# Selection masks by comparison on VectorE, indices in memory of their own, and a new order of the work around the turn, in a four-layer graph kernel

## What is computed

```python
s = jnp.sort(jnp.where(nd[..., None], x[:, None, :, :], jnp.inf), axis=2)
nv = nd.sum(2)
for tau, w in zip((0.25, 0.5, 0.75), (0.25, 0.5, 0.25)):
    pos = tau * jnp.maximum(nv - 1, 0)
    lo, hi, frac = floor(pos), ceil(pos), pos - floor(pos)
    v_lo, v_hi = s[lo], s[hi]          # taken along axis 2
    agg = agg + w * (v_lo + frac * (v_hi - v_lo))
out = x + agg
y = (relu(out @ W1 + b1) @ W2 + b2) * mask
```

## Time and profile before

| | before |
|---|---|
| time, median of 3 runs | 3453.47 us (3452.79 to 3454.65) |
| profiled execution | 3456.97 us, its span 3455.2 us |
| granted TensorE clock, mean of the span | 0.846 of full |
| PE busy | 2531.8 us, 73% |
| PE weight loads | 1180.9 us, 34% |
| DVE busy | 2743.5 us, 79% |
| ACT busy | 2210.2 us, 64% |
| chain that ended last | PE 44%, DVE 29%, ACT 17%, issue 7%, DMA 2% |

### The profile page before, as it was taken

The page is one execution under the profiler, slowest core; times in us unless marked ns, Lnnn a source line. Parts: engine busy times, 40 slices in busy tenths (PEclk is TensorE's granted clock), DMA queues, the critical chain, the costliest instruction groups (busy, mean ns, idle before and its releaser), DMA issues.

```text
span 3455.2 us, 48310 instructions
## 1 busy us (share of the span) xinstructions
PE 2531.8 (73%) x17616; PEld 1180.9 (34%) x17770; DVE 2743.5 (79%) x5221; ACT 2210.2 (64%) x3296; POOL 13.7 (0%) x24
## 2 busy tenths in 40 slices
PE   0000015688989888888989898888888898986996
PEld 0000003233333434333434333343334343333765
DVE  7999998886869788787878796878778787735776
ACT  2112434578777787878778787878777877761232
POOL 0000000000000000000000000000000000000000
PEclk6555557799999999999999999999999999997777
DMA  3002000001010101011010101010100101010011
GB/s 65 0 0 61 6 0 21 10 19 20 19 20 22 30 9 32 13 31 20 19 20 19 20 19 26 15 30 11 34 10 29 20 19 20 2 27 25 26 36 37
DMA packets 157564, 74.67 MB, mean 22 GB/s; under 512 B 125192, under 2 KB 140698, under 8 KB 157082
## 3 DMA queue, kind: packets, MB, share of 16 engines
q1 hardware_dynamic: 153210, 70.68, 8.8%
q10 hardware_dynamic: 4128, 1.05, 0.2%
HBM read 42.27 MB, written 16.83 MB: 17 GB/s over the span
## 4 chain that ended last, share of the span: by engine, by line
PE 44%; DVE 29%; ACT 17%; issue 7%; DMA 2%; SPq 0%; ACTq 0%; DVEq 0%
PE rows L621 10%; PE ring L584 8%; PE found_bank L631 6%; ACT hot L1043 5%; PE bcast L597 4%; ACT below L1008 3%; DVE keys L1305 2%; DVE keys L1306 2%; PE bcast L702 2%; PE bcast L711 2%; PE bank L873 2%; ACT prod L1036 2%; DVE delta L1347 1%; DVE delta L1345 1%; DVE perm L1349 1%
## 5 line engine op out<-in xcount | busy, mean ns | idle before, releaser
L1043 ACT ACTIVATE hot<-bcast,consts 128x1024 bf16<-128x1024 f32 x744 | 832.4, 1119 | 189.6 <-PE bcast L597 188.9
L621 PE MATMUL rows<-hot,table 128*64 128x512 bf16 x4608 | 681.2, 403 | 0.0
L584 PE MATMUL ring<-member,neigh_t 128*128 128x512 bf16 x1924 | 502.3, 402 | 61.1 <-ACT words L1000 28.7
L1036 ACT ACTIVATE prod<-rows 128x512 f32<-128x512 f32 x720 | 432.8, 601 | 46.3 <-PE rows L621 46.1
L631 PE MATMUL found_bank<-prod,consts 128*64 128x512 f32 x1536 | 410.5, 612 | 0.0
L597 PE MATMUL bcast<-idx_t,consts 32*128 32x512 f16 x1488 | 305.2, 407 | 104.9 <-ACT hot L1043 102.3
L610 PE MATMUL rows<-fine_rows,consts 32*128 32x512 bf16 x768 | 305.0, 397 | 28.5 <-DMA fine_rows<-fine_t 28.5
L521 PE MATMUL ring<-identb,adj_b 128*128 128x128 bf16 x256 | 34.6, 263 | 386.3 <-ACT adj_b L928 375.1
L584 PEld LDWEIGHTS ring<-member,neigh_t 128*128 128x128 bf16 x2048 | 187.0, 102 | 370.2 <-issue 110.2
L621 PEld LDWEIGHTS rows<-hot,table 128*64 128x64 bf16 x4608 | 210.8, 111 | 262.3 <-issue 191.3
L597 PEld LDWEIGHTS bcast<-idx_t,consts 32*128 32x128 f16 x1488 | 70.6, 91 | 491.4 <-ACT hot L1043 360.7
(11 more groups left out here) (348 smaller groups left out, 4580.9 us busy)
## 6 DMA issues: line engine op xcount, KB each, us to landing
late<-in_adj_dram SPq DMA_DIRECT2D x16, 1024.0 KB, 5.5
fine_rows<-fine_t SPq DMA_DIRECT2D x512, 24.0 KB
adjt_d<-neigh_t SPq DMA_DIRECT2D x16, 512.0 KB, 2.7
adj_l<-adjt_d SPq DMA_DIRECT2D x16, 512.0 KB, 3.6
adj_s<-adjt_d SPq DMA_DIRECT2D x16, 512.0 KB, 3.5
parts_d<-parts SPq DMA_DIRECT2D x6, 512.0 KB, 5.3
table<-parts_d SPq DMA_DIRECT2D x192, 16.0 KB, 2.2
xt_d<-keys SPq DMA_DIRECT2D x2, 1024.0 KB, 9.2
```

The source lines that it names most:

```text
L584: ins = mm(ring[u % 2][:, :], kept_t[:, j, P * i:P * i + P], member[:, j, n // 2, 512 * (n % 2):512 * (n % 2) + 512], start=(j == 0), stop ...
L621: ins = mm(rows[u % 2][C * h:C * h + C, :], table[:, s, GROUPS * h + g8, :], hot[:, u % HOT, h, :], start=False, stop=(s == 2), skip_group ...
L1036: run(prod[:, u % DEEP, :], rows[u % 2][:, :], ACT.Relu).then_inc(S["prod_by_act"], 1)
L1043: run(hot[:, u % HOT].rearrange(flat), spread_bank(l, u)[0][:, 0:2, :].rearrange(flat), ACT.Relu, bias=eq_bias[:, :]).then_inc(S["hot_read ...
```

## The change

ACT's masks go, with `edge`, `limit_ready` and `mask_made`; DVE makes them by a comparison in `select`, in a single buffer. The indices get `idx_home`, so the wait for the turn leaves tile 0 and stands in `bits_start` of the next graph. To make room fine_t, adj_l and hid_t share `turned`. The turn begins with the first fine block. SP sends fine_t in 64 DMAs instead of 32: 16 with one run per partition for plane 0 (four semaphores), then 16 for plane 1, and, when all three fine blocks are there, 32 with two runs; the ninth unit waits for the last 48 together, and adj_l is loaded after all of them. The chunks of the next first tile stand between the last units: 0 and 1 behind unit 43, then two behind each of units 44 to 46. PE sums tile 0 right behind the turn. The units are spread evenly over each tile (`share`), 22 lie in the select part, and limits(p) comes ahead of bits_last.

The core of the diff; declarations, the prologue's masks and ACT's matching order of the interleaved chunks are left out:

```diff
-LEAD = (0, 5, 10, 15, 20)
+LEAD = (0, 4, 9, 14, 22)
 SUM_AT = (4, 5, 6, 4)
 LATE = LEAD[NT]
-STEP = [LATE + n for n in (0, 1, 2, 4, 6, 7, 9, 11, 13, 15, 16, 18, 21, 23, 26, 28)]
+STEP = [LATE + n for n in (0, 1, 2, 4, 6, 7, 9, 11, 13, 14, 15, 17, 19, 21)]
 UNITS = K * GROUPS
 TURNS = K + K // 2
 BY_VECTOR = ()
 ROW_GROUP = (3, 1, 0, 2, 0, 2, 1, 3)
 ROW_SLOT = (0, 0, 0, 0, 1, 1, 1, 1)
+TURN_ORDER = (K, 0, K + 1, K + 2, 1, 2, 3, 4, 5)
...
+def share(i, s):
+
+    return LEAD[i] + (LEAD[i + 1] - LEAD[i]) * (s + 1) // 10
...
-        below = sb("below", [P, 2, TAUS, G * C], BF16)
+        below = sb("below", [P, TAUS, G * C], BF16)
...
-        idx_at, temps_at = 0, 3 * NT * K * C
-        idx = pool12[:, idx_at:idx_at + 2 * NT * K * C].bitcast(F16).rearrange("p (t k b d e) -> p t k b d e", t=NT, k=K, b=4, d=2)
-        idx_b = pool12[:, idx_at + 2 * NT * K * C:idx_at + 3 * NT * K * C].bitcast(BF16).rearrange("p (t n) -> p t n", t=NT)
+        temps_at = 3 * NT * K * C
+        idx_home = sb("idx_home", [P, 3 * NT * K * C], U16)
+        idx = idx_home[:, 0:2 * NT * K * C].bitcast(F16).rearrange("p (t k b d e) -> p t k b d e", t=NT, k=K, b=4, d=2)
+        idx_b = idx_home[:, 2 * NT * K * C:].bitcast(BF16).rearrange("p (t n) -> p t n", t=NT)
         idx_t = sb("idx_t", [P, K, N], F16)
-        fine_t = sb("fine_t", [P, 2, K // 2, N], BF16)
+        turned = sb("turned", [P, K * N], BF16)
+        fine_t = turned[:, :].rearrange("p (s q n) -> p s q n", s=2, n=N)
+        adj_l = turned[:, 0:NT * N].rearrange("p (t n) -> p t n", t=NT)
+        hid_t = turned[:, NT * N:].bitcast(F32)
...
+            def fine_part(g8, n, s, lo, hi):
+
+                slots_of = fine_rows[:, :, :].rearrange("p (q s e) n -> p q s e n", s=2, e=2)
+                row, to = s * C + 8 * g8, 32 * ROW_GROUP[g8] + 8 * n
+                return sp.dma_start(slots_of[to:to + 8, lo:hi, s, ROW_SLOT[g8], :], fine_t[row:row + 8, n, lo:hi, :])
+
             def place_fine(l):
 
-                hold(sp, S["idxT_ev"], TURNS * l + TURNS, S["sp_passed"])
+                hold(sp, S["idxT_ev"], TURNS * l + 1, S["sp_passed"])
                 if l == 0:
                     sp.wait_ge(S["cdone"], 4)
-                slots_of = fine_rows[:, :, :].rearrange("p (q s e) n -> p q s e n", s=2, e=2)
+                for g4 in range(4):
+                    for g8 in (2 * g4, 2 * g4 + 1):
+                        for n in range(2):
+                            fine_part(g8, n, 0, 0, 1).then_inc(fine_in[g4], 16)
+                for g8 in range(GROUPS):
+                    for n in range(2):
+                        fine_part(g8, n, 1, 0, 1).then_inc(S["later_in"], 16)
+                hold(sp, S["idxT_ev"], TURNS * l + 4, S["sp_passed"])
                 for s in range(2):
                     for g8 in range(GROUPS):
-                        row, to = s * C + 8 * g8, 32 * ROW_GROUP[g8]
                         for n in range(2):
-                            sp.dma_start(slots_of[to + 8 * n:to + 8 * n + 8, :, s, ROW_SLOT[g8], :],
-                                         fine_t[row:row + 8, n, :, :]).then_inc(fine_in[s][g8], 16)
+                            fine_part(g8, n, s, 1, 3).then_inc(S["later_in"], 16)
+                hold(sp, S["later_in"], 768 * l + 768, S["sp_passed"])
+                for g4 in range(4):
+                    hold(sp, fine_in[g4], 64 * l + 64, S["sp_passed"])
...
-                if u < 2 * GROUPS:
-                    pe.wait_ge(fine_in[k][g8], 32 * l + 32)
+                if u < GROUPS and u % 2 == 0:
+                    pe.wait_ge(fine_in[u // 2], 64 * l + 64)
+                if u == GROUPS:
+                    pe.wait_ge(S["later_in"], 768 * l + 768)
...
-                for u in range(TURNS):
+                for u, k in enumerate(TURN_ORDER):
...
-                units(l, 2)
                 if not b:
                     for n in range(4):
                         chunk(b, 1, n)
+                sum_first(b, 0)
+                units(l, 1)
+                sum_size(b, 0)
                 chunk(b, 1, 4)
+                units(l, 2)
+                chunk(b, 1, 5)
+                chunk(b, 1, 6)
                 units(l, 3)
-                chunk(b, 1, 5)
-                sum_first(b, 0)
-                sum_size(b, 0)
-                chunk(b, 1, 6)
+                chunk(b, 1, 7)
                 units(l, LEAD[1])
-                chunk(b, 1, 7)
                 for i in range(1, NT):
                     for s in range(10):
                         if i + 1 < NT and s < CW:
                             chunk(b, i + 1, s)
-                        units(l, min(LEAD[i] + (s + 1) // 2, LEAD[i + 1]))
+                        units(l, share(i, s))
...
-                    units(l, STEP[14])
                     pe.wait_ge(S["nv_read"], p + 1)
                     chunk(p, 0, 1)
-                    chunk(p, 0, 2)
-                    units(l, STEP[15])
-                    for n in range(3, CW):
+                for n in range(2, CW, 2):
+                    units(l, STEP[13] + n // 2)
+                    if p is not None:
                         chunk(p, 0, n)
+                        chunk(p, 0, n + 1)
...
-                    wait(act, S["mask_made"], NT * b + i - 1)
+                    wait(act, S["cnt_read"], NT * b + i - 1)
...
-            def mask(b, i, k):
-
-                if k == 0:
-                    act.wait_ge(S["limit_ready"], b + 1)
-                    act.wait_ge(S["cw_ev"], NT * CW * b + CW * i + 2)
-                    wait(act, S["mask_used"], NT * b + i - 1)
-                ins = run(below[:, i % 2, k, 0:(G - 1) * C], cnt2[:, i % 2, 0:(G - 1) * C], ACT.Sigmoid,
-                          bias=edge[:, i, k:k + 1], scale=-STEEP)
-                if k == 2:
-                    ins.then_inc(S["mask_made"], 1)
...
-                units(l, 3)
                 chunk(b, 1, 2)
                 chunk(b, 1, 3)
-                mask(b, 1, 0)
+                units(l, 3)
+                keep_sums(b, 0)
+                chunk(b, 1, 4)
                 units(l, 4)
-                chunk(b, 1, 4)
+                chunk(b, 1, 5)
+                chunk(b, 1, 6)
                 units(l, 5)
-                chunk(b, 1, 5)
-                mask(b, 1, 1)
-                keep_sums(b, 0)
-                chunk(b, 1, 6)
-                units(l, 6)
                 chunk(b, 1, 7)
-                mask(b, 1, 2)
+                units(l, LEAD[1] + 2)
                 for i in range(1, NT):
-                    level = LEAD[i] + 2
                     for s in range(10):
-                        if i + 1 < NT:
-                            if s == 2:
-                                mask(b, i + 1, 0)
-                                units(l, min(level + 1, LEAD[i + 1] + 2))
-                                mask(b, i + 1, 1)
-                                mask(b, i + 1, 2)
-                            if s < CW:
-                                chunk(b, i + 1, s)
-                        units(l, min(level + (s + 1) // 2, LEAD[i + 1] + 2))
+                        if i + 1 < NT and s < CW:
+                            chunk(b, i + 1, s)
+                        units(l, share(i, s) + 2)
...
                 for k in range(TAUS):
                     did(ts(starts[:, k, 0:last], cnt[:, 0:last], above[:, i, k:k + 1], None, ALU.is_equal))
+                for k in range(TAUS):
+                    did(ts(below[:, k, 0:last], cnt[:, 0:last], limit[:, i, k:k + 1], None, ALU.is_le))
...
+                need(count[0])
+                v.engine_nop().then_inc(S["cnt_read"], 1)
                 units(l, LEAD[i + 1])
                 need(count[0])
                 wait(dve, S["sums_ps"], 2 * (NT * b + i))
-                dve.wait_ge(S["mask_made"], NT * b + i + 1)
-                if i == 0 and b:
-                    dve.wait_ge(S["idxT_ps"], TURNS * b)
...
-            def bits_start():
-
+            def bits_start(t_of):
+
+                if t_of:
+                    dve.wait_ge(S["idxT_ps"], TURNS * t_of)
...
                     members(p, 3)
+                    limits(p)
                 units(l, STEP[12])
                 if t_of is not None:
                     bits_last()
                 if d is not None:
                     gcn_end(d)
-                if p is not None:
-                    limits(p)
```

More of the change, by code:

```diff
@@ L320, in build @@
         S = {n: sem(n) for n in names}
-        fine_in = [[sem(f"fine_in{s}_{g8}") for g8 in range(GROUPS)] for s in range(2)]
+        fine_in = [sem(f"fine_in{n}") for n in range(4)]
         adjs_in = [sem(f"adjs_in{q}") for q in range(SLOTS)]
@@ L1144, in region @@
                     chunk(p, 0, 0)
-                if d is not None:
-                    root_of(d, 2)
-                units(l, STEP[14] + 2)
-                if p is not None:
                     chunk(p, 0, 1)
-                    chunk(p, 0, 2)
-                units(l, UNITS + 2)
-                if p is not None:
```

(30 more changed lines are left out.)

28 lines of the change are left out of this document (12 added, 16 removed).

## The result

| | before | after |
|---|---|---|
| time, median of 4 runs | 3454.06 us (3452.79 to 3456.51) | 3520.47 us (3512.53 to 3525.06) |
| ratio to before, with its 95% interval | | 1.0189 (1.0169 to 1.0209) |
| profiled execution, its span | 3456.97 us, 3455.2 us | 3512.53 us, 3510.7 us |
| granted TensorE clock, mean | 0.846 | 0.834 |
| PE busy / DVE busy / ACT busy | 2531.8 / 2743.5 / 2210.2 us | 2536.8 / 2811.8 / 2005.6 us |

The change makes the kernel 66 us slower by the medians, 55.6 us in the two profiled executions, which are compared here. ACT has lost 205 us of work, and the time still went up. The chain that ended last names the place: SP's queue, which had no share worth naming before, now carries a fifth of it.

The account below looks back on a forecast made before the run. PE's order and waits bound the kernel. Per graph -2.5 us, -37 over 15 intervals, +25.5 in the last graph, +5.2 in graph 0: -6.5 on 3456.97, 3450.5; less 3.5 for the median, 3447 us. Range 3340 to 3500.

Parts of the forecast that it names:

- What bounds the kernel: In the loop, PE carries the order; an edit counts when it removes or makes a PE wait.
- The way to the gate: Without new waits PE reaches the ninth unit 39 us after the turn's first transpose, against 47.9 before.
- The gate: At the ninth unit, 64 issues of 44.4 us on SP's queue make PE wait a new 9.5 us.
- The last graph and graph 0: One-time costs: +25.5 us at the last graph's ninth unit, +5.2 us in graph 0 for VectorE's comparisons.
- Behind G: From the ninth unit's start to the next graph's first transpose: 112.36 us less 4.5 plus 1.4, giving 109.3.
- The gain of 4.5: After the ninth unit's start, shorter chunk and hot waits and two vanished VectorE waits save 4.5 us a graph.
- The cold clock: After the ninth unit's wait of 9 us, PE comes cold and loses 1.4 us a graph.
- Slower: the gate at full price: One-run issues cost 0.73 us: 3482 us, or 3529 if only mask waits after the ninth unit's start go; chance 0.27.
- The gate opens in time: One-run issues at 0.39 us leave about no wait at the ninth unit: 3288 us; at 0.50, 3365; chance 0.22.
- VectorE becomes the bound: With no wait at the ninth unit, VectorE holds the interval at 148 to 150 us: about 3310; chance 0.06.
- The third case: Same as "Slower: the gate at full price": 3482 to 3529 us; chance 0.27.

Follow-up runs that it names:

- the half gate: Kernel after the change, with the last 8 of the 64 transfers left out of the joined wait and waited for at unit 28: 3432.31 us.
- The filling: Kernel after the change, with 46 useless matmuls on TensorE ahead of the unchanged wait at the ninth unit: 3493.31 us.
- own waits: Kernel after the change, with the joined wait split into three, at the ninth unit and units 16 and 24, 16 transfers each: 3294.5 us.
- the kernel with 32 transfers: Kernel after the change, with 32 three-run transfers issued from the turn's fourth block on, a wait for each two units, none joined: 3277.67 us.
- the later count: Kernel after the change with 32 three-run transfers and no joined wait, TensorE counting the neighbours one unit later: 3257.47 us.

## Why the prediction was wrong, step by step

The forecast was 3447 us, 6.5 us faster on the profiled execution, with a range of 3340 to 3500. Measured are 3520, slower and outside the range.

**What bounds the kernel: right.** PE carries the order. That a removed or added wait of PE counts one to one was borne out by the half gate: 88 us for 93.

**The way to the gate: right.** S at T+11.2 (T+11.1 forecast), PE at the ninth unit at T+39.4 (T+39), which is G less the 10.09 us of its wait. With the gate open, G is at T+38.6.

**The gate: right, 1 us early.** Issues: 0.67 each for one run (0.66 taken), 0.73 for two (0.73 taken), 44.83 us together (44.4). The tables took 6.45 us and SP was free 0.6 us later than worked out. G is T+49.5 (T+48.5). The prediction took a rule of the Trainium skill (*SBUF — State Buffer*, section The DMA setup-cost knee) for the price of an issue: the fixed part of a DMA doesn't depend on its bytes. The page means mostly the time until the data has landed, of which the issue is a small part, so it doesn't state a price for the queue. As for that price, the trace shows 0.73 us for two runs as for three, and 0.06 us less for one. An unchanged price would have given 46.6 us.

**The last graph and graph 0: right.** +26.7 for 25.5, +3.3 for 5.2.

**Behind G: this step failed.** I had taken 4.5 us off and put 1.4 us on, -3.1 together. The mean shows +0.5. The term breaks up in two, and a run stands behind each.
- *The gain of 4.5 is 2.2 when the gate is open* (111.8 to 109.55). In the mean of 13 graphs the chunk wait of 0.7 went; the hot waits fell by 1.2 (4.6 to 3.4), not by 2.2; the two waits for VectorE stayed, 1.7 us where they were 1.4. Less time at the lower clock (6.3 to 4.7 us a graph) gives another 0.8, which the prediction didn't have. I had argued that VectorE runs further ahead. It does, and it then stands 4 to 6 us at the transfer of the adjacency, where it hardly waited before (2.5 us in 13 graphs): PE's wait stays and only its source changes. The prediction gives no row on what releases VectorE there. VectorE's waits in the trace show the hand-over, and moving PE's count one unit later took PE's two waits away.
- *The cold clock costs 2.7, not 1.4* (112.3 against 109.55). I had counted the slow lookups right behind the wait and the chunk next to them. 1.4 us lost would be 2.8 us at the lower level; the mean is 5.5. The filling gives 1.75 back and leaves 1.8 us more at the lower level than with own waits, which at half speed is the rest. Why 1.3 us of these lie 40 to 70 us behind G is open.

Per graph that is 2.3 + 1.3 from behind G and 1.0 from the gate, 4.6 us; the mean of 13 intervals rose by 2.0 where -2.5 was forecast, 4.5 apart. That is 58 us; the first and the last of the 15 intervals (-0.7 and -0.3 measured) add 4, and the two ends take 1 off (1.2 - 1.9). Together it is the whole error of 62 us on the profiled execution, 3512.5 against 3450.5. The median of the runs lies 8 us above that execution.

**The rivals.** *Slower: the gate at full price* gave 3482 to 3529 and holds the measured time, but half for another reason: the mean price was 0.70, under the 0.705 from which it was to decide, and what decided was its second half, that a PE that comes late finds the waits again. That isn't quite it either: the waits are there whether PE comes late or not. *The gate opens in time* gave 3288 without the cold stretch. The kernel with own waits, where the gate is open by another means, took 3294.5, so this side of the sum was sound, though the price of an issue stayed where the forecast had it. *VectorE becomes the bound* was to be about 3310 with an interval of 148 to 150. With the gate open the interval was 148.1, inside it; but VectorE was busy 130.7 us of that in the kernel with 32 transfers, and in the run with the later count the interval came down to 146.6 with VectorE still waiting 4.5 us a graph for the transfer. So it didn't bind.

**The chances.** The forecast stood 0.011 us in the price of an issue away from the slower case, and the term behind G had a spread of 3 to 6 us of gain. A gain near zero there, which 15 graphs turn into 47 us, wasn't in the range of the forecast. The third case had it, with 0.27.

**What the parts are worth.** On the kernel before: masks on VectorE -87 us, turn order and early transfers another -47; with the indices' own memory (3), the spacing (22), the interleaved chunks and the earlier sums (not tried apart) it is -178 in all (3277.7 against 3455.8), and the later count makes it -197. The 64 transfers with their joined wait cost 105 us on the kernel before, with the turn order, and 243 us (3520.5 less 3277.7) on the one that has the rest, 226 of them the joining, since a gate fixed by SP's queue at T+49.5 leaves nothing of what is gained ahead of it.

## What to carry to other kernels

A wait joined over many transfers puts the consumer at the end of the issuing queue: count the issues between the consumer's first need and the last transfer in the group, times the issue time of that form, and compare with when the consumer arrives. One semaphore for each group that is first read together gave 226 us here, at no other change. When a wait is for another engine, see what that engine waits for in the new order. Here VectorE came earlier and PE's wait stayed, because a transfer that hangs on PE's own work took its place; what took the wait away was other work put between.

## What the runs showed of the hardware

- Issue times on SP, from SBUF to SBUF with 8 partitions: one run of 1 KB for each 0.67 us (21.39 for 32), two runs 0.73 (44.83 less 21.39), three runs 0.73 (23.30 for 32). Splitting a transfer nearly doubles the queue's time.
- PE stood for 10.1 us without a matmul; from 1659.00 to 1665.70 the granted clock was 0.50, the lower level of 1.2 GHz, and it stayed there for 3.25 us of matmuls behind the wait before it was 1.00 again. A PE kept busy with 46 useless matmuls stood at 1.00 in both places, and the kernel was 27 us faster for it. The Trainium skill (*TensorE: Matmul & The Clock Gate*, Part 1) describes a clock that falls to half when the engine stands idle; this trace agrees.
- A wait of 4.9 us (half of the gate) left 4.7 us at the lower level behind it, one of 10.6 us left 5.5 (means of 13 graphs): halving the wait didn't save the clock.
- Stretches at 0.50 also come behind matmuls, 40 to 70 us behind G, as 1710.80 to 1713.30 in the kernel after and 1621.90 to 1625.10 with own waits; no run here says why.
